# Layer norm terms per group of batches: the first inside stage one, the second inside the attention stage

## The reference, cut to what matters

```python
def _layernorm(x, axis=-1, eps=1e-05):
    m = jnp.mean(x, axis=axis, keepdims=True)
    v = jnp.var(x, axis=axis, keepdims=True)
    return (x - m) / jnp.sqrt(v + eps)

h = _L0_tok_ref(x, ...)                        # x: 128 x 256 x 192, h: 128 x 127 x 192
h = h + _L0_attn_ref(_layernorm(h), ...)       # 8 heads, three softmaxes over key pairs, projection
h = h + _L0_ffn_ref(_layernorm(h), ...)        # router picks one of 4 experts, 192 -> 192 -> 192
```

## Time and profile before

| | us |
|---|---|
| median of 3 runs | 2066.68 (2065.92 to 2067.2) |
| the profiled execution | 2065.83 |
| its span, first to last instruction | 2063.9 |

### The profile page before, as it was taken

The page is one execution under the profiler, slowest core; times in us unless marked ns, Lnnn a source line. Parts: engine busy times, 40 slices in busy tenths (PEclk is TensorE's granted clock), DMA queues, the critical chain, the costliest instruction groups (busy, mean ns, idle before and its releaser), DMA issues. The chain is left out here.

```text
span 2063.9 us, 60351 instructions
## 1 busy us (share of the span) xinstructions
PE 1911.3 (93%) x20800; PEld 1179.2 (57%) x20800; DVE 1478.8 (72%) x3636; ACT 1410.4 (68%) x2978; POOL 1162.1 (56%) x2198
## 2 busy tenths in 40 slices
PE   3999999993999999999999999999991899999998
PEld 3999999980444444444444444444441566666666
DVE  4555555553899999999999999999981455555554
ACT  1333333330889899899898998998982666666665
POOL 1111111127677777777777777777756565565561
PEclk9999999995999999999999999999996899999999
DMA  4444444421444444444444444444440332322322
GB/s 138 127 114 117 121 122 122 122 62 29 80 89 89 88 90 88 90 88 90 90 86 90 90 90 89 89 88 90 87 80 13 57 64 62 71 62 63 71 63 52
DMA packets 512122, 176.03 MB, mean 85 GB/s; under 512 B 452169, under 2 KB 511308, under 8 KB 512076
## 3 DMA queue, kind: packets, MB, share of 16 engines
q1 hardware_dynamic: 512075, 175.43, 38.7%
HBM read 53.79 MB, written 12.48 MB: 32 GB/s over the span
## 5 line engine op out<-in xcount | busy, mean ns | idle before, releaser
L692 DVE TENSOR_REDUCE tops<-p_maxa 128x6 f32<-128x762 f32 x512 | 483.0, 943 | 61.9 <-PE p_maxa L534 60.7
L605 PE MATMUL p_o<-probs,vn 127*32 127x256 f32 x6144 | 410.7, 385 | 0.2 <-DVE att L720 0.2
L530 PE MATMUL p_s<-qm,kt 32*128 32x256 f16 x3072 | 399.1, 275 | 1.3 <-ACT probs L649 0.4
L646 ACT ACTIVATE probs<-p_s 128x512 f32<-128x512 f32 x512 | 305.4, 596 | 108.4 <-PE p_s L530 95.6
L694 DVE TENSOR_REDUCE tops<-p_maxb 128x4 f32<-128x508 f32 x512 | 346.4, 676 | 0.0
L652 ACT ACTIVATE probs<-p_s 128x512 f32<-128x512 f32 x512 | 309.4, 604 | 0.0
L649 ACT ACTIVATE probs<-p_s 128x512 f32<-128x512 f32 x512 | 304.9, 596 | 0.3 <-PE p_s L530 0.2
L966 DVE TENSOR_TENSOR gel_lo<-gel,gel_hi 128x512 f16<-128x512 f32 x192 | 147.4, 768 | 215.7 <-ACT gel_hi L956 214.4
L534 PE MATMUL p_maxa<-kt,qt 24*128 24x256 f16 (+1 forms) x2048 | 284.1, 250 | 16.0 <-DMA kt<-qk 8.5
L360 POOL TENSOR_TENSOR diag<-ident,weight 128x256 f32<-128x256 f32 x128 | 78.9, 617 | 369.2 <-DVE band L339 328.3
L530 PEld LDWEIGHTS p_s<-qm,kt 32*128 32x128 f16 x3072 | 134.7, 91 | 182.9 <-issue 168.6
(11 more groups left out here) (186 smaller groups left out, 4522.3 us busy)
## 6 DMA issues: line engine op xcount, KB each, us to landing
xn<-in_xn SPq DMA_DIRECT2D x32, 768.0 KB, 6.3
xt_a<-in_xt SPq DMA_DIRECT2D x32, 512.0 KB, 4.4
out<-out_sb SPq DMA_DIRECT2D x32, 336.0 KB, 2.7
xt_b<-in_xt SPq DMA_DIRECT2D x32, 256.0 KB, 5.2
xt<-hx SPq DMA_TRANSPOSE x128, 2.3
kt<-qk SPq DMA_TRANSPOSE x128, 2.7
qt<-qk SPq DMA_TRANSPOSE x128, 2.4
qm<-qk SPq DMA_TRANSPOSE x128, 2.7
```

Source lines behind the costliest of these rows:

```text
L530: return nc.tensor.matmul(o, kt[full(j), r, kind, g, :], qm[full(j), r % 2, versions, g, :], start=True, stop=True, skip_group_check=True)
L605: last = nc.tensor.matmul(p_o[32 * j:32 * j + 32, blocks, :], vn[0:NP, r, src:src + 32], probs[0:NP, r % 2, QUAD * g + j, kind * 256:(kind ...
L646: nc.scalar.activation(probs[:, r % 2, h + 1, 0:512], p_s[1][:, :, :].rearrange("p x n -> p (x n)"), ACT.Exp, scale=SCALE).then_inc(act_e1 ...
L692: nc.vector.tensor_reduce(top[:, q, pair, 4:10], p_ma[:, 0:6, 0:NP], AX.X, ALU.max, negate=True).then_inc(dve_ma[u], 1)
```

## The change

`norm_terms` and both its calls are removed, with `t.stats`; `t.half` (the exponent) shrinks to four columns.

In stage one DVE keeps the statistics of two groups in a ring. In iteration i it makes the terms of group i - 3, spread over the steps: three instructions in k = 1, three in k = 2, two in k = 3, each on four columns. POOL makes the power in its step k = 2, behind that step's `diag`.

In the attention stage DVE follows bn_stats with a wait for it and with bn_aggr, which gives mean and variance in one instruction, into `moments` for four batches. Once in four iterations (r = 2) POOL turns the four into rstd and shift, with six instructions at the end of its iteration. In the next iteration (r = 3) DVE waits for POOL's result before it goes on, since it will overwrite `moments`. The wait for dve_h stands ahead of maxima(i, r, 0) now.

```diff
@@ tokenize, vector
+            def terms(i, par, step):
+                g = i - 3
...
+                if step == 1:
+                    dve.wait_ge(dve_stats, seen((i - 2) * G))
...
+                    nc.vector.tensor_tensor(mean[:, :], st[:, :, 1], st[:, :, 4], ALU.add)
+                    nc.vector.tensor_tensor(gap[:, :], st[:, :, 1], st[:, :, 4], ALU.subtract)
+                    nc.vector.tensor_tensor(var[:, :], st[:, :, 2], st[:, :, 5], ALU.add).then_inc(dve_norm, 1)
+                elif step == 2:
+                    dve.wait_ge(dve_norm, seen((i - 2) * 4 - 3))
+                    nc.vector.tensor_tensor(gap[:, :], gap[:, :], gap[:, :], ALU.mult)
+                    nc.vector.tensor_scalar(var[:, :], var[:, :], 1.0 / C, EPS, ALU.mult, ALU.add).then_inc(dve_norm, 1)
+                    dve.wait_ge(dve_norm, seen((i - 2) * 4 - 2))
+                    nc.vector.scalar_tensor_tensor(out=var[:, :], in0=gap[:, :], scalar=0.25, in1=var[:, :],
+                                                   op0=ALU.mult, op1=ALU.add).then_inc(dve_norm, 1)
+                elif step == 3:
+                    dve.wait_ge(pool_root, seen(i - 2))
+                    nc.vector.tensor_copy(t.rstd[:, bass.ds(g * G, G)], root[:, :])
+                    nc.vector.scalar_tensor_tensor(out=t.shift[:, bass.ds(g * G, G)], in0=mean[:, :], scalar=-0.5, in1=root[:, :],
+                                                   op0=ALU.mult, op1=ALU.mult).then_inc(dve_norm, 1)
@@ tokenize, gpsimd
+                    if k == 2 and within(i - 3, NG):
+                        pool.wait_ge(dve_norm, seen((i - 2) * 4 - 1))
+                        nc.gpsimd.tensor_tensor(root[:, :], var[:, :], t.half[:, :], ALU.pow).then_inc(pool_root, 1)
@@ attend, vector
             def body(i, r):
+                if within(i - 3, NB):
+                    dve.wait_ge(dve_h, seen(i - 2))
+                    dve.wait_ge(dve_aggr, seen(i - 3))
                 maxima(i, r, 0)
                 if within(i - 3, NB):
-                    dve.wait_ge(dve_h, seen(i - 2))
-                    nc.vector.bn_stats(t.stats[:, bass.ds((i - 3) * 6, 6)], t.h[:, bass.ds((i - 3) * C, C)])
+                    nc.vector.bn_stats(stats[:, :], t.h[:, bass.ds((i - 3) * C, C)]).then_inc(dve_stats, 1)
+                    dve.wait_ge(dve_stats, seen(i - 2))
+                    if r == 3:
+                        dve.wait_ge(pool_norm, seen(i - 3))
 
                 maxima(i, r, 1)
+                if within(i - 3, NB):
+                    nc.vector.bn_aggr(moments[:, (r + 1) % U, :], stats[:, :]).then_inc(dve_aggr, 1)
@@ attend, gpsimd
+            def terms(i, r):
+
+                if r == 2 and within(i - 3, NB):
+                    pool.wait_ge(dve_aggr, seen(i - 2))
+                    nc.gpsimd.tensor_tensor(varied[:, :], moments[:, :, 1], eps[:, :], ALU.add).then_inc(pool_norm, 1)
+                    nc.gpsimd.tensor_tensor(neg[:, :], moments[:, :, 0], minus[:, :], ALU.mult)
+                    pool.wait_ge(pool_norm, seen(i - 5))
+                    nc.gpsimd.tensor_tensor(root[:, :], varied[:, :], t.half[:, :], ALU.pow).then_inc(pool_norm, 1)
+                    pool.wait_ge(pool_norm, seen(i - 4))
+                    nc.gpsimd.tensor_tensor(spare[:, :], root[:, :], one[:, :].broadcast_to([128, U]), ALU.mult)
+                    nc.gpsimd.tensor_tensor(t.rstd[:, bass.ds(i - 6, U)], root[:, :], one[:, :].broadcast_to([128, U]), ALU.mult)
+                    nc.gpsimd.tensor_tensor(t.shift[:, bass.ds(i - 6, U)], neg[:, :], root[:, :], ALU.mult).then_inc(pool_norm, 2)
@@ audio_tower
-        norm_terms(nc, t, NB, "first_")
         attend(nc, t, NB)
-        norm_terms(nc, t, NB, "second_")
```

More of the change, by code:

```diff
@@ L173, in tokenize @@
         pe_att, act_att, pe_h, act_h = sem("pe_att"), sem("act_att"), sem("pe_h"), sem("act_h")
-        dve_stats = sem("dve_stats")
+        stats = sb("stats", [128, 2, G, 6])
+        mean, gap, var, root = (sb(x, [128, G]) for x in ("mean", "gap", "var", "root"))
+        dve_stats, dve_norm, pool_root = sem("dve_stats"), sem("dve_norm"), sem("pool_root")
         block = ctx.enter_context(nc.Block())
@@ L342, in body @@
                         last.then_inc(dve_band, 1)
+                    terms(i, par, k)
                     u = n - 2 * G - 1
                     if within(u, NB):
+                        q, kk = (par, k - 1) if k else (1 - par, G - 1)
                         dve.wait_ge(act_h, seen(u + 1))
-                        nc.vector.bn_stats(t.stats[:, bass.ds(u * 6, 6)], t.h[:, bass.ds(u * C, C)]).then_inc(dve_stats, 1)
+                        nc.vector.bn_stats(stats[:, q, kk, :], t.h[:, bass.ds(u * C, C)]).then_inc(dve_stats, 1)
             loop(dve, body)
@@ L423, in attend @@
         one = sb("one", [128, 1])
+        stats, moments = sb("att_stats", [128, 6]), sb("moments", [128, U, 2])
+        varied, root, spare, neg = (sb(x, [128, U]) for x in ("varied", "att_root", "spare", "negated"))
+        eps, minus = sb("eps", [128, U]), sb("minus", [128, U])
         ones16 = sb("ones16", [128, 128], F16)
@@ L732, in _ @@
             nc.gpsimd.memset(one[:, :], 1.0)
+            nc.gpsimd.memset(eps[:, :], EPS)
+            nc.gpsimd.memset(minus[:, :], -1.0)
+            def terms(i, r):
[9 more added lines that the diff above has]
+                    nc.gpsimd.tensor_tensor(t.shift[:, bass.ds(i - 6, U)], neg[:, :], root[:, :], ALU.mult).then_inc(pool_norm, 2)
             def halves(i, r):
@@ L777, in body @@
                     nc.gpsimd.tensor_tensor(ay[:, C:2 * C], att[:, :], ay[:, 0:C], ALU.subtract).then_inc(pool_y, 1)
+                terms(i, r)
             loop(pool, body)
@@ L1045, in audio_tower @@
         t.h = sb("h", [128, NB * C])
-        t.stats = sb("stats", [128, NB * 6])
         t.rstd = sb("rstd", [128, NB])
         t.shift = sb("shift", [128, NB])
-        t.half = sb("half", [128, NB])
+        t.half = sb("half", [128, G])
         t.ident = sb("ident", [128, 128])
```

31 lines of the change are left out of this document (6 added, 25 removed).

## The result

The changed kernel took 2144.17 us (median of 4 runs, 2142.34 to 2156.22), the kernel before 2066.54 us beside it. The ratio is 1.039, with a 95% interval from 1.0357 to 1.0422: 78 us slower. The prediction was 2075.5 us with a range up to 2097. It had the sign, and it was 69 us short. The profiled execution is the slowest of the four, 2156.22 us with a span of 2154.5 us and a mean granted clock of 0.949. The other three took 2142 to 2144 us at 0.956 to 0.959; a fifth on record, which is not in the median, took 2148.48 us at 0.954.

The account below looks back on a forecast made before the run. A loop through ACT, POOL, transposes and PE, with a PE-VectorE loop almost level, was taken to bound the attention stage. The terms -42.3 + 42.3 + 9 = +9 us on 2066.7 gave 2075.5 us, range 2056 to 2097.

Parts of the forecast that it names:

- Part 1: The gaps after stage one and after the attention stage shrink by 21.0 and 21.3 us, total -42.3 us.
- Part 2: Stage one's loop: VectorE's added instructions and POOL's power cost nothing, the power with 0.7 us to spare.
- Part 3: Attention loop, every fourth iteration: VectorE waits for POOL's terms, 1.57 us late; 1.41 us lost 30 times, +42.3 us.
- Part 4: Attention loop, every iteration: the wait for bn_stats and disturbed minima cost 0.29 us a round, +9 us (0 to 20).
- the clock gives nothing back: At the two gaps: no gain from the granted clock, since PE still idles over 8 us there.
- (c): POOL's power has its own start-up of 0.8 us or so; each round loses 2.2 us: 2099; chance 0.13.
- (a): Attention loop: wait behind bn_stats and bn_aggr cost nothing, only the stall stands against the gain: 2066.7, no change; chance 0.15.
- (b): Attention loop: POOL's chain is short, 1.1 us instead of 1.65; faster, 2051, with extras 2060; chance 0.12.
- (d): Attention loop: collisions with L768 and bn_aggr delay the third unit's maxima, 0.2 us over 96 iterations: 2094; chance 0.08.
- (e): POOL's power costs about the same whatever its size; 20.8 us chains return: some 600 us longer; chance 0.02.

Follow-up runs that it names:

- the best versions: The early release with aggregation and waits at the iteration's end: 2037.87 us; POOL's chain also moved, 2040.44 us; without the extra written-out round, 2036.37 us.
- the product: The changed kernel with a product in place of POOL's power in the attention stage: 2080.33 us, ratio 1.0067.
- the early release: The changed kernel, but VectorE waits in every fourth iteration only until POOL has read the moments: 2057.48 us, ratio 0.9954.
- the extra matmuls: The changed kernel with nine extra 128x512 matmuls on TensorE where it stands still in every fourth iteration: 2127.41 us, ratio 1.0284.
- the run with both waits later: The early release with both VectorE waits ahead of the minima instead of the second head group's maximum, and the aggregation behind the minima: 2053.76 us, ratio 0.9942.

## Why the prediction was wrong

**Part 1 was right.** The gaps shrank by 21.1 and 21.0 us; the forecast was 21.0 and 21.3.

**Part 2 was right to 1 us.** The stage-one loop from its first to its last bn_stats takes 406.1 us in place of 405.0. POOL's power now waits 172 us in all for the variance, but POOL's wait for VectorE's band falls from 328 to 133 us at the same time: it is idle time that POOL had.

**Part 3 had the mechanism and was some 30% too small.** It said 1.57 us of lateness on VectorE and 1.41 on the loop; measured are 2.04 and 1.98. Three terms of VectorE's lateness were small. The power on 4 columns takes 1.01 to 1.02 us, not 0.83, and the whole chain 1.90, not 1.65. POOL begins it 0.31 us after bn_stats and not 0.15: it ran later in this iteration than in the earlier trace rows. And VectorE starts 0.09 us after the chain's end, not 0.03. The 0.16 us of slack that I took off for TensorE's p_maxb of u2 were there. In the iteration of 1036 us it starts 0.05 after the maximum that frees it:

```profile
1039.31 0.68 DVE L699 TENSOR_REDUCE tops<-p_maxb 128x4 f32<-128x508 f32 x1
...
1040.04 0.39 PE L539 MATMUL p_maxb<-kt,qt 24*128 24x256 f16 x1
```

That is 3.90 us after bn_stats (1036.14) where it was 2.02 before (1030.96 and 1032.98), so 1.88 = 2.04 - 0.16. The last 0.10 of the 1.98 arise behind it. Where the clock is kept, 5.96 us pass from the first matmul of qkv to the next bn_stats, and 5.86 in the kernel before. Over 30 rounds the part costs 59 us instead of 42.

**Part 4 was small as well.** The three iterations outside the stall lose 0.50 us a round, 15 us in all; the part said 9. Where i mod 4 = 2 the loss is 0.14, as the wait for bn_stats was priced (0.13), and the pair of runs that differ in this wait alone confirms it with 0.14. Where i mod 4 is 0 and 1 each iteration lost 0.12 us more than I gave it. Of this 0.10 is again the stretch from the first matmul of qkv to the next bn_stats (5.96 instead of 5.86), and it is not the wait: the version without it has most of this loss too (8.27 and 8.13 instead of 8.15 and 8.03). Where i mod 4 = 3 the wait would cost 0.36 us if the longer wait for POOL did not cover it.

**The step that failed outright is the sentence that the clock gives nothing back.** I asked it of the two gaps only. (The reading behind it was also a little off: the window of the earlier trace rows begins 1.3 us and ends 4.3 us after the last bn_stats of stage one, not 2 and 5.) I never asked it of the new standstill in the loop, and yet rows 8 show how the clock falls soon after TensorE stops. The loop of the kernel before had a TensorE that never stood still and a clock of 1.00:

```profile
600.00:900.00 300.00, 299.96 (x4080) 138.47 (x4080) 281.39 (x556) 270.13 (x556) 223.42 (x446) 1.00 0.44 89
```

Part 3 itself put 1.4 us of standing still into every fourth iteration. This missing term is some 43 to 45 us in the median, and it makes up most of the miss: 17 + 6 + 45 = 68 of 69 us. (By the prediction's own terms 2066.7 + 9 is 2075.7, not 2075.5.)

**Rivals.** (c) had the power's start-up in it, in part (0.39 us instead of 0.8), and alone it would have given less than it claimed. (a) would have needed a free wait behind bn_stats. The Trainium skill (VectorE: DVE Perf Modes, "The DRAIN you can't avoid") says that a semaphore between two VectorE instructions costs nothing extra. Here the measurement goes against it, with a start 0.38 us after bn_stats instead of 0.27 and 17 us in the time. (b), (d) and (e) did not come about. The chain was longer. From 600 to 1500 us the minima took over 0.3 us instead of 0.2 more often than before (78 of 294 against 55 of 333) but lost less each time, 17 us against 19 in all. And a power of 4 columns takes 1.01 us, not 20.8.

What stays open: why rounds at the full clock still take 32.73 to 32.84 us in the best versions instead of 32.41, most of it in the iteration with i mod 4 = 3 (8.41 to 8.44 instead of 8.20), the 0.10 us ahead of the next bn_stats in three iterations of four, and why the half with the first stage alone has rounds of 32.6 us. Why a round of the changed kernel has now no low clock, now 3.4 and now 6.8 us of it after standstills of the same length is open too.

## What to carry to other kernels

Where TensorE is busy without a break, price a new wait twice: once for its length on the path, and once for what the granted clock does after the standstill. Here 1.65 us of idle time cost 2 us more on average when the clock fell, and 0.97 us of it almost never brought the clock down. Release a buffer when it has been read, not when the whole chain that reads it is done, and put new small work where its engine already waits: nearly the same instructions went from 78 us slower than before to 31 us faster by an earlier release and by moving two waits and one instruction. An engine without idle time pays for a wait for its own result.

## What the hardware did that was not expected

- With a standstill of 1.46 to 1.80 us of TensorE (1.65 in most) the granted clock was at half in 26 of 30 rounds, for 3.4 or 6.8 us; with 0.97 us (the product) in 1 of 30; with the 0.5 to 0.65 us of the early release and of the extra matmuls in none of the rounds between the first and the last.
- A POOL power costs 0.39 us and 0.159 us a column of 128 partitions, a POOL product of 4 columns 0.20 us. A bn_aggr of one bn_stats takes 0.17 us, and the next VectorE instruction starts 0.09 us (a maximum, in the run with both waits later) or 0.12 us (a minimum, in the changed kernel) after its start.
- A wait of VectorE for the result of its own 0.35 us bn_stats delays the next instruction by 0.11 us, from 0.27 to 0.38 us after the start.
- Writing out four more iterations ahead of the loop made the first three rounds 4 us longer, with one standstill of TensorE of 1.6 to 1.7 us and 3.4 us at the low clock among them.
